# Routed tiles of a mixture-of-experts kernel taken in pairs, their weight copies moved from GpSimd to VectorE and ScalarE

## What is computed

```python
x = x + attn(cond(x, itok_B_0_15))
xf = cond2(x, itok_B_0_3)                      # low rank (16) per language + embedding
ys = geglu(xf @ Ws1 + bs1) @ Ws2 + bs2         # shared expert, 512 hidden
top_val, top_idx = top_k((xf @ Wr + br) / TAU, 2)
w = softmax(top_val)
yr = sum over the two chosen e of w_e * (geglu(xf @ We1[e] + be1[e]) @ We2[e] + be2[e])   # 768 hidden
x = x + ys + yr
```

## Time and profile before

| | us |
|---|---|
| runs of the kernel before | 806.34, 805.82, 805.70 (median 805.82) |
| the profiled execution, its own time | 806.17 |
| its span in the trace, first to last instruction | 804.4 |
| routed stage, first layer of tile 0 to the last scatter | 434.39 to 797.53 |
| granted clock of TensorE over the span | 0.996 |

### The profile page before, as it was taken

How to read it: one execution, slowest core, us unless ns; L and a number is a source line. 1 busy time by engine, 2 the same in 40 slices (tenths; PEclk the granted TensorE clock), 3 DMA queues, 4 the chain that set the end, 5 groups by cost and what they waited for, 6 DMA issues and landing times.

```text
span 804.4 us, 27682 instructions
## 1 busy us (share of the span) xinstructions
PE 783.6 (97%) x9379; PEld 658.2 (82%) x9380; DVE 575.9 (72%) x1350; ACT 294.3 (37%) x883; POOL 405.4 (50%) x511
## 2 busy tenths in 40 slices
PE   7999999999999999999999999999999999999994
PEld 6788888888888888777778888888888888888883
DVE  2999877777777777679884676666666666666661
ACT  1444444444444444542222333333333333333330
POOL 3133244444444444401012777777777777777762
PEclk9999999999999999999999999999999999999998
DMA  9553355555565554048734233223222322232222
GB/s 277 153 187 101 112 170 180 182 174 177 180 182 181 182 182 146 2 158 232 231 130 139 28 42 37 33 35 39 35 34 33 38 38 33 34 40 36 33 31 26
DMA packets 49325, 86.11 MB, mean 107 GB/s; under 512 B 7298, under 2 KB 27970, under 8 KB 49122
## 3 DMA queue, kind: packets, MB, share of 16 engines
q1 hardware_dynamic: 33778, 68.83, 27.2%
q0 software_dynamic: 13888, 15.13, 14.3%
q10 hardware_dynamic: 1584, 1.10, 0.5%
HBM read 68.48 MB, written 16.55 MB: 106 GB/s over the span
## 4 chain that ended last, share of the span: by engine, by line
PE 90%; DVE 5%; issue 2%; DMA 1%; SPq 0%; POOL 0%; ACT 0%; DVEq 0%
PE ps L1575 24%; PE ps L1562 13%; PE ps L1234 7%; PE ps L1473 6%; PE ps L1332 4%; PE ps L1556 4%; PE ps L1306 3%; PE ps L1250 3%; PE ps L1279 3%; PE ps L1462 3%; PE ps L1219 3%; PE ps L1543 2%; PE ps L1339 2%; PE ps L1292 2%; PE ps L1321 2%
## 5 line engine op out<-in xcount | busy, mean ns | idle before, releaser
L1575 PE MATMUL ps<-arena,stage 128*128 x900 | 206.6, 379 | 0.0
L1575 PEld LDWEIGHTS ps<-arena,stage 128*128 128x128 f32 x900 | 165.2, 190 | 19.5
L504 POOL DMA_INDIRECT out_dram<-stage,to_row x75 | 120.6, 1609 | 76.0 <-DVE stage L1143 71.3
L708 ACT ACTIVATE stage<-ps 128x384 f32<-128x384 f32 x150 | 65.4, 488 | 241.6 <-PE ps L1562 241.6
L1562 PE MATMUL ps<-token_rows,token_rows_T 64*128 64x128 f32 x1800 | 129.2, 272 | 0.0
L1562 PEld LDWEIGHTS ps<-token_rows,token_rows_T 64*128 64x128 f32 x1800 | 118.8, 188 | 1.7
L496 POOL DMA_INDIRECT token_rows<-gated_rows,from_row x75 | 75.1, 1001 | 61.6 <-DVE to_row L1022 38.9
L1117 DVE COPY token_rows<-ps 128x128 f32<-128x128 f32 x75 | 21.9, 292 | 111.8 <-PE ps L1544 111.8
L408 POOL TENSOR_TENSOR arena<-arena 128x256 f32<-128x256 f32 x32 | 23.4, 732 | 139.3 <-DVE arena L832 132.3
L1127 DVE TENSOR_TENSOR stage<-ps,stage 128x384 f32<-128x384 f32 x150 | 76.0, 549 | 1.8 <-ACT stage L708 1.8
L795 DVE TENSOR_REDUCE arena<-ps 128x8 f32<-128x512 f32 x64 | 43.9, 686 | 42.4 <-PE ps L1270 42.0
(11 more groups left out here) (173 smaller groups left out, 1473.8 us busy)
## 6 DMA issues: line engine op xcount, KB each, us to landing
stage<-in_we_dram SPq DMA_DIRECT2D x36, 512.0 KB, 4.7
arena<-in_cond_w_dram SPq DMA_DIRECT2D x64, 256.0 KB, 2.8
arena<-in_we_dram SPq DMA_DIRECT2D x12, 768.0 KB, 6.0
arena<-in_x_both_dram SPq DMA_DIRECT2D x31, 256.0 KB, 2.7
arena<-in_L_cond_bias_dram SPq DMA_DIRECT2D x64, 64.0 KB, 2.9
out_dram<-arena SPq DMA_DIRECT2D x32, 128.0 KB, 2.7
be_bc<-in_be_rows_dram SPq DMA_DIRECT2D x13, 192.0 KB, 3.4
gated_rows<-token_rows POOLq DMA_DIRECT2D x2, 1152.0 KB, 11.6
```

The source lines that it names most:

```text
L504: pool.indirect_dma_start(out_rows, bass.IndirectOffsetOnAxis(to_row[:, t:t + 1], 0), y_sb[t % YR], None, compute_op=ALU.add).then_inc(d_a ...
L708: nc.scalar.activation(g_sb[hf].rearrange("p (j n) -> p j n", n=P), first_out[1][:, :, hf, :], ACT.Gelu).then_inc(g_ok, 1)
L1575: last = mm(ps[:, 4 + s % 2, 0:D], actT_sb[s % 2][:, hf, j * P:(j + 1) * P], arena[:, ds(e * E2 + (NJ * hf + j) * D, D)], start=(hf == 0 a ...
```

## The change

- TensorE takes two tiles at a time (t odd): `first_layer(t)`, `first_layer(t + 1)`, `rows_transpose(t + 2)`, `rows_transpose(t + 3)`, `second_layer(t - 2)`, `second_layer(t - 1)`. For this the first layer has two places in banks 0 to 5, chosen by the tile's parity, the transposes have two places in bank 7, the second layer writes banks 6 and 7, and a third `actT_sb` lies in the weights of the shared expert. The two places meet in banks 1 and 4, so the gelu of an odd tile waits for the first column block of the next tile (`h_first`), and `first_layer` of an odd tile waits for both tiles of the pair before to be multiplied.
- Block j = 2 of the weight copies goes to VectorE and the bias copy to ScalarE. GpSimd does one scatter and one gather a tile and nothing else. It gathers 12 tiles ahead (RING = 12), and the loops run over 12 tiles.
- The last two tiles are written out: `first_layer(73)`, `second_layer(71)`, `first_layer(74)`, then the second layers of 72, 73 and 74.
- At the joint three transposes, instead of two, stand before `first_layer(1)`, and the last unit of the shared expert goes to banks 6 and 7.

The diff, cut (removed lines stand in full above):

```diff
@@ -29,7 +29,7 @@
-RING = 6
+RING = 12
 YR = 3
...
+        actT_sb.append(ws2[:, 0:NJ, :].rearrange("p k n -> p (k n)").rearrange("p (h n) -> p h n", h=2))
         y_sb = [cut(D) for _ in range(YR)]
...
+        hidden_ps = ps[:, 0:6, :].rearrange("p b n -> p (b n)").rearrange(
+            "p (g s j h n) -> p s g j h n", g=2, s=2, h=2, n=P)
+        def first_out(t, s):
+            return hidden_ps[:, 0 if s % 2 == 1 or isinstance(t, int) and t == 0 else 1]
+        last_shared = [ps[:, 6, 0:D], ps[:, 7, 0:D]]
...
-                pool.wait_ge(d_dummy, 16)
...
-            def copy_last(t):
-                copy_first(pool, nc.gpsimd.tensor_copy, t, t, 2)
-                e = pool.value_load(expert_of[0:1, ds(t, 1)], min_val=0, max_val=NE - 1)
-                nc.gpsimd.tensor_copy(w1bx[t % 2].bitcast(bf16), w1b[:, ds(e * (NJ * P), NJ * P)]).then_inc(w1bx_ok, 1)
-            for s in range(RING):
+            for s in range(RING // 2):
                 load_rows(s, s)
...
+            for s in range(RING // 2, RING):
+                load_rows(s, s)
+            pool.wait_ge(d_dummy, 16)
             pool.wait_ge(d_out_low, 16 * low_tiles)
             pool.wait_ge(d_out_high, 16 * (NT - low_tiles))
+            def next_rows(t):
+                if t + RING < NS:
+                    load_rows(t + RING, t % RING)
             for t in range(NS):
...
+                add_rows(t, t % RING)
+                next_rows(t)
...
-            def gelus(t, s):
+            def gelus(t, s, turn_of=None):
                 act.wait_ge(h_ps, t + 1)
+                if s % 2 == 1:
+                    act.wait_ge(h_first, turn_of)
                 for hf in range(2):
+                    if not isinstance(t, int) or t > 0:
+                        act.wait_ge(act_ok, 2 * t + (hf - 1))
+                    nc.scalar.activation(g_sb[hf].rearrange("p (j n) -> p j n", n=P), first_out(t, s)[:, 1, :, hf, :],
                                          ACT.Gelu).then_inc(g_ok, 1)
...
+            def tile_weights(t, s):
+                copy_first(act, copy, t, s, 0)
+                e = act.value_load(expert_of[0:1, ds(t, 1)], min_val=0, max_val=NE - 1)
+                copy(w1bx[s % 2].bitcast(bf16), w1b[:, ds(e * (NJ * P), NJ * P)]).then_inc(w1bx_ok, 1)
+            def two_tiles(t, k, q):
+                for d in range(2):
+                    gelus(t + d, k + d, RING // 2 * q + (k + 1) // 2)
+                    if not (isinstance(t, int) and t + d + 2 >= NS):
+                        tile_weights(t + d + 2, k + d + 2)
+                for d in (4, 5):
+                    if not (isinstance(t, int) and t + d >= NS):
+                        widen(t + d, (k + d) % RING, 16 * q + 16 * ((k + d) // RING) + 16)
...
+            act.wait_ge(l_cut, 4 * (NE + 1))
...
+            widen(2, 2, 16)
+            gelus(0, 0)
+            tile_weights(2, 2)
+            for t in (3, 4):
+                widen(t, t, 16)
...
+            def rowT_copy(t, s, ready):
+                at = D * (1 - s % 2)
+                dve.wait_ge(rowT_ps, ready)
+                V.tensor_copy(s_rowT[s % 2], ps[:, 7, at:at + P])
...
+            def multiply(t, s):
+                for hf in range(2):
+                    dve.wait_ge(g_ok, 2 * t + (hf + 1))
+                    if hf == 0 and isinstance(t, int) and t < 3:
+                        dve.wait_ge(shy_ps, NT - 2 if t == 0 else NT)
+                    elif hf == 0:
+                        dve.wait_ge(y_ps, t - 2)
+                    V.tensor_tensor(actT_sb[s % 3][:, hf, :].rearrange("p (j n) -> p j n", n=P),
+                                    first_out(t, s)[:, 0, :, hf, :], g_sb[hf].rearrange("p (j n) -> p j n", n=P),
+                                    ALU.mult).then_inc(act_ok, 1)
+            def tile_weights(t, s):
+                for j in (1, 2):
+                    copy_first(dve, V.tensor_copy, t, s, j)
...
+            def combine_last(v):
+                n = NT - 2 + v
+                dve.wait_ge(shy_ps, n + 1)
+                V.tensor_tensor(x2res[:, ds(n * D, D)], x2res[:, ds(n * D, D)], last_shared[v], ALU.add).then_inc(comb_ok, 1)
+            def two_tiles(t, k):
+                known = isinstance(t, int)
+                multiply(t, k)
+                if not (known and t + 2 >= NS):
+                    for d in (2, 3):
+                        rowT_copy(t + d, (k + d) % RING, t + 4)
+                    tile_weights(t + 2, k)
+                if not (known and t == 1):
+                    gate_bias(t - 2, (k - 2) % RING)
+                gate_bias(t - 1, (k - 1) % RING)
+                if not (known and t == 1):
+                    add_bias(t - 2, (k - 2) % RING)
+                multiply(t + 1, k + 1)
+                if not (known and t + 2 >= NS):
+                    tile_weights(t + 3, k + 1)
+                add_bias(t - 1, (k - 1) % RING)
...
+                tile_weights(t, t)
             for v in range(2):
                 combine(TOK // U - 2, v, 0)
+            for t in (1, 2):
+                rowT_copy(t, t, 3)
+            multiply(0, 0)
+            tile_weights(2, 2)
+            for v in range(2):
+                combine_last(v)
             dve.wait_ge(d_be2, 16)
+            for k in range(1, RING, 2):
+                two_tiles(k, k)
             with dve.Fori(1, NS // RING) as q:
+                for k in range(1, RING, 2):
+                    two_tiles(RING * q + k, k)
+            two_tiles(NS - 2, 1)
+            for t in (NS - 2, NS - 1):
+                gate_bias(t, t % RING)
+            for t in (NS - 2, NS - 1):
+                add_bias(t, t % RING)
...
             def rows_transpose(t, s):
+                at = D * (1 - s % 2)
                 pe.wait_ge(wide_ok, t + 1)
-                if not isinstance(t, int) or t > 0:
-                    pe.wait_ge(rowT_sb, t)
+                if isinstance(t, int) and t == 3:
+                    pe.wait_ge(comb_ok, NT)
+                elif not (isinstance(t, int) and t < 5) and s % 2 == 1:
+                    pe.wait_ge(y_ok, t - 4)
+                tr(ps[:, 7, at:at + P], s_wide[s % 2][:, 0:P], ident)
+                tr(ps[:, 7, at + P:at + 2 * P], s_wide[s % 2][:, P:2 * P], ident).then_inc(rowT_ps, 1)
             def first_layer(t, s):
                 pe.wait_ge(rowT_sb, t + 1)
-                if not isinstance(t, int) or t > 0:
-                    pe.wait_ge(act_ok, 2 * t)
+                if isinstance(t, int) and t == 0:
+                    pe.wait_ge(sha_ok, 2 * (TOK // U))
+                    pe.wait_ge(comb_ok, NT - 3)
+                elif isinstance(t, int) and t == 2:
+                    pe.wait_ge(comb_ok, NT - 2)
+                    pe.wait_ge(act_ok, 2)
                 else:
-                    pe.wait_ge(sha_ok, 2 * (TOK // U))
+                    pe.wait_ge(act_ok, 2 * t if s % 2 == 1 else 2 * t - 2)
                 pe.wait_ge(w1bx_ok, t + 1)
...
+                    if j == 0 and s % 2 == 0 and not (isinstance(t, int) and t == 0):
+                        last.then_inc(h_first, 1)
                 last.then_inc(h_ps, 1)
-            def second_layer(t, s, e):
+            def second_layer(t, s):
+                e = pe.value_load(expert_of[0:1, ds(t, 1)], min_val=0, max_val=NE - 1)
+                bank = 6 if s % 2 == 1 or isinstance(t, int) and t == 0 else 7
+                if not (isinstance(t, int) and t == 0):
+                    pe.wait_ge(y_ok, max(t - 1, 1) if isinstance(t, int) else t - 1)
+                if bank == 7:
+                    pe.wait_ge(rowT_sb, min(t + 5, NS) if isinstance(t, int) else t + 5)
                 for hf in range(2):
                     pe.wait_ge(act_ok, 2 * t + (hf + 1))
                     for j in range(NJ):
+                        last = mm(ps[:, bank, 0:D], actT_sb[s % 3][:, hf, j * P:(j + 1) * P],
...
+            def two_tiles(t, k):
+                known = isinstance(t, int)
+                for d in (0, 1):
+                    first_layer(t + d, k + d)
+                for d in (2, 3):
+                    if not (known and t + d >= NS):
+                        rows_transpose(t + d, (k + d) % RING)
+                for d in (2, 1):
+                    if not (known and t < d):
+                        second_layer(t - d, (k - d) % RING)
             rows_transpose(0, 0)
             shared_out(TOK // U - 2, 0)
             first_layer(0, 0)
+            for t in (1, 2):
+                rows_transpose(t, t)
+            shared_out(TOK // U - 1, 1, into=last_shared)
             pe.wait_ge(d_w2, 16 * NE)
             pe.wait_ge(r_done, 1)
+            for k in range(1, RING, 2):
+                two_tiles(k, k)
             with pe.Fori(1, NS // RING) as q:
+                for k in range(1, RING, 2):
+                    two_tiles(RING * q + k, k)
+            first_layer(NS - 2, 1)
+            second_layer(NS - 4, RING - 1)
+            first_layer(NS - 1, 2)
+            for t in (NS - 3, NS - 2, NS - 1):
```

(1 more changed line is left out.)

113 lines of the change are left out of this document (22 added, 91 removed).

## The result

The changed kernel takes 812.73 us (median of 4 runs, 811.01 to 813.90) against 805.76 of the kernel before on the same chip: a ratio of 1.0082, 95% interval 1.0070 to 1.0094. It is 0.8% slower. Forecast were 804.2 in a range of 802.2 to 809.6. The profiled execution took 811.84, of which 1.8 lie outside the span.

What follows compares the result with a forecast made beforehand. TensorE was taken as the bound, losing 0.26 us a tile, with the scatters' chain 0.1 from binding. Terms -8.9 + 1 - 0.2 + 6.3 = -1.8 from 806.17 gave 804.4, adjusted to 804.2 us; range 802.2 to 809.6.

Steps and rivals of the forecast that it cites:

- (a): TensorE's turns between 128 and 64 rows, one instead of two in two tiles: 35 pairs take 322.6, not 331.5; -8.9 us.
- (b): VectorE's path to the next pair: multiply done 8.6 to 9.0 after X, the pair's first-layer start; +1 us.
- Rival 3: VectorE's path to the even tile's multiply becomes the bound: 809.6 us at 9.4 a pair, 816.6 at 9.6; chance 0.28.
- (c): ScalarE's bias copy, GpSimd's removed copies, twelve gathers ahead and loops of twelve tiles: 0 each.
- (d): The joint: tile 1 starts at 441.3, tile 3 at 449.2, -0.2 us; tile 1's scatter moves to 457.8.
- (e): The end: last scatter starts 22.9 behind tile 73's first layer instead of 16.55, with three spacings of 4.63; +6.3 us.
- The other road: The scatters' chain by itself: 457.8 + 73 x 4.63 = 795.8 for the last scatter, -1.7 against 797.53.
- rival 4: Scatters' chain runs at 4.66 with its late landings, so the stage gains nothing: 806.4 us; chance 0.10.
- rival 2: Scatters land sooner or start sooner behind a landing, 4.5 or less a spacing: 802.8 us; chance 0.15.
- Both roads: The summed terms (-1.8) and the scatters' chain (-1.7) agree, so TensorE and the scatters end level.

Runs made afterwards that it cites:

- a_one_copy_w: Changed kernel with VectorE's two weight copies a tile merged behind one register load, TensorE's third wait kept: 807.01 us, ratio 1.0013 to the kernel before.
- a_gpsimd: Changed kernel with the third weight block's copy and the bias copy back on GpSimd: 811.19 us, ratio 1.0072 to the kernel before.
- b_moved: Kernel before, in its own order, with only GpSimd's two copies a tile moved to VectorE and ScalarE: 805.71 us, ratio 1.0000.
- b_ring12: Kernel before with only twelve row buffers and loops of twelve tiles: 805.45 us, ratio 0.9993.
- a_ring6: Changed kernel with loops of six tiles and six gathers ahead, as before the change: 1073.87 us, ratio 1.3331 to the kernel before.

## Why the prediction was wrong, step by step

**(a)** Right. An undisturbed pair takes 9.21, and where nothing disturbs them, 35 of them take 322.4 (a_one_copy_w: 447.53 to 769.9), 9.1 under the 331.5 of before.

**(b)** The mechanism was right, the size wrong: +5.3 instead of +1, 0.15 a pair, inside the bounds of 0 to 0.4. The loads were taken as 0.66 to 0.77 apart; the two scaled biases came 0.77 to 0.87 apart in most pairs and up to 1.15, the second at X+7.2 to 7.9 (8.3 in one pair) instead of 6.9 to 7.3. So the path ended at X+8.9 to 9.1 in the pairs that went well, and any disturbance showed. The blocking, for which the +0.03 stood, is nearly gone. Rival 3 (chance 0.28) was this, and at 9.37 it says 777.2 for tile 73, which is what came. It says 800.1 for the last scatter, 1.8 too early, since it holds the pairs and not the chain for the bound. The Trainium skill's lock ("SBUF — State Buffer", Who interferes with whom) shows once more in a_gpsimd, where VectorE's copy takes 0.65 beside GpSimd's copies and 0.30 without them. Its other side, VectorE's copies that lengthen scatters, does not show here: the median scatter takes 1.59 in the changed kernel, with twice the copies on VectorE, against 1.61 before and 1.60 in a_gpsimd.

**(c)** ScalarE's bias copy and the moved copies are 0 (b_moved, in the old order). "Twelve gathers ahead: 0" and "loops of twelve tiles: 0" were wrong as prices: 1.2 in the closing drain, and a late multiply at four turns, some 0.3 to 0.8 of pair time each.

**(d)** Right: 441.52 against 441.3, 449.31 against 449.2, scatter 1 at 457.99 against 457.8.

**(e)** Too small, and for the wrong reason. The last scatter starts 24.7 behind tile 73 instead of 22.9, so the term is +8.2 instead of +6.3. The three spacings were 4.55, a little shorter than assumed. But scatter 71 did not wait for its result, ready at 785.82: it waited for scatter 70 and started 2.5 later. The whole chain was late, not only its end.

**The other road was the failing step.** I priced the chain at 4.63, from two scatters and the median landing. A chain adds up means. Over 73 spacings the landing was 3.90 and the time from landing to next start 0.81, 4.71 together: 457.99 + 343.95 = 801.94. That is 0.08 over the 4.63, and the prediction itself named 0.03 as what it could bear. The mean of before, 3.87, could be had from its 75 landings, and with the 0.79 between landing and start it gives 4.66, rival 4 (806.4). The rest are late landings (5.4 and 5.8 for scatters 1 and 8) and late starts; why these two landed late stays open. In rival 2 I wrote that landings keep to 3.6 to 3.8, but these are the shortest and the median of the earlier trace rows, whose longest is 5.2. "Both roads say the same" was therefore no support: both were under-priced, the first by 4.3 in (b) and 1.8 in (e), the chain by 6.0. The chain's 6.0, 0.2 at its start and 1.2 in the drain make the miss of 7.4 in the profiled execution. Shown by taking away: 8.4 for the queue of the last four, 5.7 for VectorE's loads (3.0 of it by an earlier start of the chain), 13.7 for both.

**What was not seen at all**: that the chain kept the scatters away from the gathers. Rival 2, the nearest to a freer chain (spacings of 4.5), gave 802.8. Really freeing the scatters gave 828.4, 9.3 of it from a late start of the stage, until the gathers were moved.

## What to carry to other kernels

If a serial chain of DMAs has a tenth of a microsecond to spare per turn, a change that makes the engines faster can hand the kernel over to it: price the chain with the mean over all its turns, and ask from where it starts and how many turns stand behind the last result. Ask also what these turns carry: here the last seven belonged to padding. Count register loads as work on the engine that issues them; merging two copies behind one load was worth 5.7 us here, moving copies between engines nothing that can be told from noise. A wait taken away moves the work behind it: look at what it will now meet.

## What the hardware showed unexpectedly

- ScalarE's gelu started 0.9 to 1.6 behind the end of the block it waited for, as long as GpSimd ran scatter, gather and scatter 0.30 apart; with the gather elsewhere, 0.1. Which resource that is stays open.
- In three of the programs TensorE stood still for 5 us inside the shared expert, with nothing waited for, and then had 1.2 GHz for 6.8 us; their near twins had neither. A difference of up to 7 us between variants can be this: compare where a stage starts before comparing times.
- From landing to the start of the next scatter pass 0.79 at the median in the changed kernel, and 0.79 or less in nine of ten turns; the longest was 1.56.
- Twelve row buffers, with loops of twelve tiles, instead of six lengthen GpSimd's closing drain from 2.68 to 3.90 (b_ring12), and six of each in the changed kernel bring it back from 3.91 to 2.69 (a_ring6). Which of the two does it was not tried.
